# Sparse products of a graph kernel: a ring of 40 gather slots, index columns read in place, one wait per 20 gathers

## What is computed

```python
def prop(z):
    return jax.ops.segment_sum(edge_weight[:, None] * z[src], dst, num_segments=N_SUP)
for i in range(L):                       # L = 5
    z = h @ W[i] + b[i]
    x_start = prop(z)
    xi = h
    for _ in range(RHP):                 # RHP = 5
        xi = (prop(xi) + x_start) / (2.0 + GAMA)
    mean = jnp.mean(xi, axis=0)
    var = jnp.var(xi, axis=0)
    out = gamma[i] * (xi - mean) / jnp.sqrt(var + BN_EPS) + beta[i]
    h = jnp.where(out > 0, out, LEAKY_SLOPE * out)
```

## Time and profile before

| | us |
|---|---|
| median of 3 runs | 13111.46 |
| lowest and highest run | 13095.41, 13116.89 |
| span of the profiled execution, first to last instruction | 11598.4 |
| median less span | 1513.1 |
| first to last start of the 5,000 gathers of the sparse products | 1326.5 to 9009.6 |

### The profile page before, as it was taken

How to read it: one execution, slowest core, us unless ns; L and a number is a source line. 1 busy time by engine, 2 the same in 40 slices (tenths; PEclk the granted TensorE clock), 3 DMA queues, 4 the chain that set the end, 5 groups by cost and what they waited for, 6 DMA issues and landing times. The chain is left out here.

```text
span 11598.4 us, 175759 instructions
## 1 busy us (share of the span) xinstructions
PE 7734.7 (67%) x38121; PEld 5090.7 (44%) x38121; DVE 6797.1 (59%) x24532; ACT 1197.8 (10%) x2596; POOL 7123.4 (61%) x7294
## 2 busy tenths in 40 slices
PE   4633377788777797777877778877779177660090
PEld 2423233357333475333663345743337055560070
DVE  5644655567555576555665556765556666450176
ACT  0122000001000011000010000100000511440005
POOL 5756366663666664666636666456666466766664
PEclk8755555679555697555785556965559578785555
DMA  3133354432444424444334444244543522662106
GB/s 126 44 126 142 91 91 92 92 70 69 92 92 92 90 49 95 91 92 92 61 76 93 92 92 81 58 95 92 91 93 52 178 62 63 174 174 36 24 28 268
DMA packets 1057829, 1076.56 MB, mean 93 GB/s; under 512 B 193805, under 2 KB 913982, under 8 KB 1057648
## 3 DMA queue, kind: packets, MB, share of 16 engines
q0 software_dynamic: 211200, 395.39, 22.0%
q1 hardware_dynamic: 723504, 525.23, 14.3%
q10 hardware_dynamic: 123072, 155.41, 4.3%
HBM read 565.26 MB, written 522.63 MB: 94 GB/s over the span
## 5 line engine op out<-in xcount | busy, mean ns | idle before, releaser
L864 POOL DMA_INDIRECT G<-tab,ridx x5000 | 4746.3, 949 | 3013.2 <-issue 2328.4
L981 PE MATMUL PS<-G,lring 128*1 128x128 f32 x10000 | 2411.0, 361 | 1504.0 <-DMA G<-tab,ridx 1470.1
L356 DVE SCALAR_TENSOR_TENSOR G<-G,whole,PS 1x128 f32<-1x128 f32 (+1 forms) x4050 | 1353.8, 334 | 2568.5 <-PE PS L981 1977.4
L995 PE MATMUL PS<-G,M 128*128 128x128 f32 x10000 | 2780.8, 418 | 45.5 <-DVE G L356 44.0
L995 PEld LDWEIGHTS PS<-G,M 128*128 128x128 f32 x10000 | 2155.6, 274 | 684.6 <-issue 376.4
L981 PEld LDWEIGHTS PS<-G,lring 128*1 128x1 f32 x10000 | 556.1, 85 | 3071.0 <-DMA G<-tab,ridx 2721.0
L377 DVE TENSOR_SCALAR M<-keyrow,keycol,wccol 128x128 f32 (+1 forms) x5004 | 1393.6, 350 | 1.0
L956 ACT COPY big<-PS 128x512 f32 x250 | 146.4, 585 | 7147.2 <-PE PS L991 7147.2
L688 ACT ACTIVATE big<-big,nb,rs 128x128 f32<-128x128 f32 x1564 | 614.8, 479 | 935.4 <-POOL nb L679 911.8
L948 DVE TENSOR_TENSOR Y<-PS,big 128x512 f32<-128x512 f32 x1000 | 679.4, 679 | 0.0
L356 DVE SCALAR_TENSOR_TENSOR carry<-G,whole,PS 1x128 f32<-1x128 f32 (+1 forms) x1350 | 451.2, 334 | 182.0 <-DVE G L356 0.3
(11 more groups left out here) (387 smaller groups left out, 9973.5 us busy)
## 6 DMA issues: line engine op xcount, KB each, us to landing
tab<-Y SPq DMA_DIRECT2D x1250, 256.0 KB, 3.1
G<-tab,ridx POOLq DMA_INDIRECT x5000, 3.3
big<-agg SPq DMA_DIRECT2D x90, 832.0 KB, 6.4
x<-big ACTq DMA_DIRECT2D x60, 832.0 KB, 3.6
big<-x SPq DMA_DIRECT2D x60, 832.0 KB, 4.8
xt_d<-big ACTq DMA_DIRECT2D x30, 858.0 KB, 7.7
x2n<-big ACTq DMA_DIRECT2D x30, 838.5 KB, 3.5
big<-x2n SPq DMA_DIRECT2D x30, 838.5 KB, 5.3
```

Of the source, the lines that this page charges most:

```text
L356: nc.vector.scalar_tensor_tensor(carried if jj == GR else row0(j), row0(j - 1), whole[0:1, bass.ds(tile + jj - 1, 1)], local(jj - 1), ALU. ...
L864: pool.indirect_dma_start(G[:, j, 0:D], None, tab_in(k), bass.IndirectOffsetOnAxis(ap=ridx[:, j:j + 1], axis=0)).then_inc(l_got[j], 16)
L981: nc.tensor.matmul(PS[0:1, CAR, j % GR, :], lring[:, j:j + 1], G[:, j, 0:D], start=True, stop=True).then_inc(l_row, 1)
L995: ins = nc.tensor.matmul(PS[:, SUM + h, j % GR, :], M[:, j, :], G[:, j, 0:D], start=True, stop=True)
```

## The change

`G` gets 40 slots (RG) in place of 8. POOL's program for a product is written out as 200 gathers without a loop: slot and index column are constants, the columns are read from `gidx` itself, and DVE's copy into `ridx` and the semaphore `l_idx` are gone. POOL waits once in 20 gathers, on `l_sum` alone, with a credit of LEAD = 5 groups in place of 2. DVE's and PE's loops now have passes of 40 tiles (10 groups), 5 to a product, in place of 25 passes of 8. Later phases place some of their tiles in the part of `G` that they do not use (`spare`).

```diff
-        G = sb("G", [P, U, D + HEADS])
+        G = sb("G", [P, RG, D + HEADS])
...
-            with pool.Fori(0, IT) as i:
-                for j in range(U):
-                    g = 2 * (r0 + i) + j // GR
-                    steady(pool, g + 1)
-                    if j % GR == 0:
-                        pool.wait_ge(l_idx, g + 1)
-                        pool.wait_ge(l_sum, g + 1)
-                    pool.indirect_dma_start(G[:, j, 0:D], None, tab_in(k), bass.IndirectOffsetOnAxis(
-                        ap=ridx[:, j:j + 1], axis=0)).then_inc(l_got[j], 16)
+            for t in range(T):
+                if t % (RG // 2) == 0:
+                    steady(pool, g0 + t // GR + 1)
+                    pool.wait_ge(l_sum, g0 + t // GR + 1)
+                pool.indirect_dma_start(G[:, t % RG, 0:D], None, tab_in(k), bass.IndirectOffsetOnAxis(
+                    ap=gidx[:, t:t + 1], axis=0)).then_inc(l_got[t % RG], 16)
...
-            with dve.Fori(0, IT) as i:
-                for h in range(2):
-                    g = 2 * (r0 + i) + h
-                    running_sums(dve, g, U * i + GR * h, h, lambda j: G[0:1, j, 0:D],
+            with dve.Fori(0, LI) as i:
+                for q in range(NG):
+                    h, g, tile = q % 2, g0 + NG * i + q, RG * i + GR * q
+                    running_sums(dve, g, tile, 0, lambda j, q=q: G[0:1, GR * q + j, 0:D],
                                  lambda jj: PS[0:1, CAR, jj, :], carry[:, 0:D], l_row, l_ch)
...
-                    nc.vector.tensor_copy(ridx[:, GR * h:GR * h + GR],
-                                          gidx[:, bass.ds(U * i + U + GR * h, GR)]).then_inc(l_idx, 1)
...
-                    dve.wait_ge(l_sum, g + 3)
+                    dve.wait_ge(l_sum, g + LEAD + 1)
...
-            with pe.Fori(0, IT) as i:
-                for h in range(2):
+            with pe.Fori(0, LI) as i:
+                for q in range(NG):
...
-                credit(l_sum, 2)
+                credit(l_sum, LEAD)
```

More of the change, by code:

```diff
@@ L38 @@
 TG = T // 2
+RG = 40
+NG = RG // GR
+LEAD = NG // 2
+LI = T // RG
 TP = T + U
@@ L821, in build @@
         ZB_, HZB = (PA, PA + 1), (PB, PC)
-        l_w, l_wr, l_col, l_base, l_idx, l_mask, l_lr, l_ch, l_row, l_sum, l_ev, l_xt, l_xc, l_yl, l_sq = (
-            sem("l_" + n) for n in "w wr col base idx mask lr ch row sum ev xt xc yl sq".split())
-        l_got = pool_sems("l_got", U)
+        l_w, l_wr, l_col, l_base, l_mask, l_lr, l_ch, l_row, l_sum, l_ev, l_xt, l_xc, l_yl, l_sq = (
+            sem("l_" + n) for n in "w wr col base mask lr ch row sum ev xt xc yl sq".split())
+        l_got = pool_sems("l_got", RG)
         l_tab, l_u, l_h, l_z, l_hz = (sems("l_" + n, 2) for n in "tab u h z hz".split())
@@ L967, in l1_pe @@
         def l1_pe(pe, l, k):
-            r0 = rounds(l, k)
+            g0 = 2 * rounds(l, k)
             last = k == NL - 1
-            with pe.Fori(0, IT) as i:
-                for h in range(2):
[L972 to L977, removed]
+            with pe.Fori(0, LI) as i:
+                for q in range(NG):
+                    h, g, tile = q % 2, g0 + NG * i + q, RG * i + GR * q
+                    gl = 2 * IT * l + NG * i + q
+                    for j in range(GR):
+                        s = GR * q + j
+                        if j == 0:
@@ L978, in l1_pe @@
                             pe.wait_ge(l_lr, g + 1)
                             pe.wait_ge(l_ch, OPS * g + 1)
[L980 to L981 removed]
+                        pe.wait_ge(l_got[s], 16 * (LI * (NL * l + k) + i) + 16)
+                        nc.tensor.matmul(PS[0:1, CAR, j, :], lring[:, GR * h + j:GR * h + j + 1], G[:, s, 0:D],
                                          start=True, stop=True).then_inc(l_row, 1)
[L983 to L984 removed]
+                    for j in range(GR):
+                        s = GR * q + j
+                        if j == 0:
@@ L999, in l1_pe @@
                         pe.wait_ge(l_sq, gl)
-                        node_sums(pe, U * i + GR * (h - 1), 1 - h)
+                        node_sums(pe, tile - GR, 1 - h)
             if last:
@@ L1615, in build @@
         xts = big[:, 0:T * XW].rearrange("p (t f) -> p t f", f=XW)
-        AL = sb("AL", [P, T, HEADS])
+        spare = G[:].rearrange("p s f -> p (s f)")[:, U * (D + HEADS):]
+        AL = spare[:, 0:T * HEADS].rearrange("p (t h) -> p t h", h=HEADS)
         AD = sb("AD", [P, U, HEADS])
@@ L1665, in build @@
         HG = 2 * HEADS
-        ALT = sb("ALT", [TG, 2, HEADS, P])
-        FW = sb("FW", [TG, 2, HEADS, P])
-        pen = sb("pen", [TG, 2, P])
+        ALT, FW = (spare[0:TG, 800 + 1024 * k:1824 + 1024 * k].rearrange("p (g h i) -> p g h i", g=2, h=HEADS)
+                   for k in range(2))
+        pen = spare[0:TG, 2848:3104].rearrange("p (g i) -> p g i", g=2)
         tpen = sb("tpen", [TG, 2, HEADS])
@@ L1677, in _ @@
             def _(dve):
-                a2 = AL[:].rearrange("p t h -> p (t h)")
+                a2 = spare[:, 0:T * HEADS]
                 link(dve, "dve", nc.vector.scalar_tensor_tensor(a2, a2, 0.2, a2, ALU.mult, ALU.max))
```

36 lines of the change are left out of this document (18 added, 18 removed).

## The result

| | before | changed |
|---|---|---|
| median, us | 13112.56 (4 runs, 13095.41 to 13116.89) | 15297.74 (4 runs, 15272.18 to 15304.69) |
| ratio | | 1.1662 [1.1646, 1.1678] |
| span of the profiled execution, us | 11598.4 | 15302.9 |

The forecast was 12,546 us, faster. The kernel became 2,185 us slower, far outside the range. The profiled execution of the changed kernel took 15,304.69 us by the clock of the runs, 1.8 us more than its span. Nothing of 1,513 us lies around it, and that is the first sign of what went wrong.

The account below looks back on a forecast made before the run. The prediction took POOL's issue of gathers in the sparse products as the bound: 13,111 us less 470 (20 products) and 95 (five last products) gave 12,546 us, all else 0; 8-in-10 range about 12,390 to 12,790 us.

Parts of the forecast that it names:

- The base: Sum: the 1,513 us between profiled span and median taken as unchanged, the gain subtracted from the median of 13,111 us.
- PE and DVE are faster than POOL: Products, data at hand: PE 4.2 us a group, DVE 3.6, POOL's four gathers 5.02, so POOL's issue is the bound.
- rival 2: Products: PE and DVE need the 5.48 us a group they take now, so any ring gives 13,111 us; chance 0.04.
- The wait is met when POOL comes to it; I take 0: POOL's wait once in 20 gathers: already met, 0 us; if late each time, 6 us a product.
- The 10.3 us from the last gather of a product to the first of the next stay: Switch between products: landing, last group on PE and DVE, and store form a chain the change does not touch.
- The four products of a layer at 250.5 us, the last at 269.5: Gathers of 20 products from 274 to 250.5 us, 470 us gained; five last ones to 269.5 including turn, 95 us.
- Index column: DVE loses 1,250 index copies, covered by its waits for PE: 0; 90 us in all if DVE were the bound.
- satisfied wait: 190 of 200 gathers lose an already met wait: 0 taken, bounds 0 and 0.23 us a gather, 1,150 us in all.
- loop: POOL's gathers written out without a loop: branches fall at gathers that wait anyway, 0 us.
- rival 1: The gather's 0.30 us gap goes with its wait, PE becomes the bound: 11,896 us; chance 0.06.
- Longer passes on DVE and PE: Jumps back over DVE's 302 instructions, 125 in all, up to 2.74 us each, covered by 8 us of slack: 0.
- The slower rival: Last products: PE falls to its low clock for a share of their 250 groups, up to 13,501 us; chance 0.04.

Follow-up runs that it names:

- b0: Kernel before, unchanged, run again with a profile on a slow chip: 13,093.29 us, span 13,091.5.
- e3: Changed kernel with POOL's wait at every fourth gather in place of every twentieth, slow chip: 13,301.86 us.
- e14: Changed kernel with a wait at every fourth gather and POOL up to nine groups ahead, slow chip: 13,644.31 us, ratio 1.038.
- e10: The file of e3 (changed kernel, wait at every fourth gather) run again on a slow chip: 13,305.3 us.
- a0: Changed kernel, unchanged, run again on a slow chip: 15,043.81 us, ratio 1.1524.
- e16: Changed kernel, unchanged, on the same slow chip as e14: 15,376.86 us, ratio 1.1699.
- e7: Changed kernel with a wait at every fourth gather and POOL held to two groups ahead, quick chip: 11,586.85 us.
- e13: The file of e7 (changed kernel, two groups ahead) on a slow chip: 13,106.38 us, ratio 1.0045.
- e4: Changed kernel with PE counting `l_row` up twice a group in place of four times, quick chip: 11,104.55 us.
- e2: Kernel before without the satisfied wait on three of four gathers, slow chip: 13,044.77 us.
- e1: Changed kernel with the satisfied wait before each gather put back, slow chip: 15,043.28 us, ratio 1.1515.
- e8: The file of e4 (changed kernel, two `l_row` updates a group) on a slow chip: 15,069.0 us.
- e12: Changed kernel with a one-column copy on POOL behind each gather, slow chip: 14,637.17 us, ratio 1.1209.
- e9: The file of e1 (changed kernel, satisfied wait before each gather) run again on a slow chip: 15,026.13 us.

## Why the prediction was wrong

**The base.** The step that failed first is the sum's: "I take what lies around the span as unchanged and set the gain against the median". The difference of 1,513 us was not launch and end, which take 1.8 us. It was mostly idle time inside the stages, which my profile did not have. By the b0 profile the products take 305 and 376 us on average in place of 274 and 277, which is 1,113 us of it. The first gather comes 95 us later, what follows the last one takes 263 us longer, and the turns make up most of the rest. This step did not make the forecast's size wrong by itself, as the runs were its base; it hid that the kernel was bound by something else. A gap of 12% between a span and its runs was a finding, and I used it as a constant.

**"PE and DVE are faster than POOL."** This holds for their own work: 3.8 us a group when nothing holds them, less than the 4.2 that I worked out for the low clock. It fails for the hand-over between them, for which I had no term at all. On a slow chip it limits the kernel before to 6.1 us a group (305 us by 50), against the 5.02 of POOL's issue. A larger ring gained nothing there (e3 and e14), and that alone is rival 2, "PE and DVE need what they take now", with a chance of 0.04.

**"The wait is met when POOL comes to it; I take 0."** This is the term that failed by the most. It was wrong on the slow chips: POOL waited 13.4 and 14.1 us at its 20th gathers, 3,308 us in 200 waits. One wait in 20 gathers was costed for the chance that it is met late, never for what 20 gathers in a row do to the others. e10 against a0, and e14 against e16, put the price of that step at about 1,740 us, and e7 and e13 clear all other parts.

**"The 10.3 us from the last gather of a product to the first of the next stay."** The change does touch that chain. POOL ends a product several groups ahead of PE, and the backlog makes 33 us of it on a slow chip. Of the 1,959 us by which the span of a0 exceeds that of b0, the 20 products take 1,000 from first to last gather, these 20 switches 420, the five last products 361 and the turns behind them 153.

**The four products of a layer at 250.5 us, the last at 269.5.** On the quick chip e4 has 250.75 and 254.8 us from the first gather to the end of the last, and its last products take 267 to 270 us up to the turn. With the switches of 12 to 16.5 us in place of 11, the gain was 496 us where the sum had 565. The 250.5 was right. The last product's closing was right in kind, and PE kept a clock of 0.96. e4 differs from the changed kernel in two updates a group, which changed nothing on a slow chip. The changed kernel itself never ran on the quick chip, so its time there is argued and not shown.

**Index column, satisfied wait, loop: 0 each.** Right by e2 and e1 (the wait) and by e13, at 0.45% for all together. The gap of 0.30 us stays without the wait, so rival 1 fell.

**Longer passes on DVE and PE.** Mostly right. Fetches of instructions grew from 42 to 254 on the page's queue q14:

```profile
q14 instruction: 254, 2.07, 0.0%
```

By the rule that the prediction cites it had every pass end in a fetch. The trace shows them in two products of layer 1 and in one of each later layer (24 to 26 of the 254 packets each, 3 to 5 in most others). In a0 these six take 362 to 375 us, the other products but the last ones 347 to 354. That is what the Trainium skill warns of on the page "Runtime: NRT & Kernel Launch", section "Instruction fetch mechanics". It was no part of the main loss, and no run separated it from other differences between products. With the cover that e4 has on the quick chip only its first product took longer, 258 us in place of 250 to 253. Without it, in e7, the six took 275 to 287 us, the others 270 to 274.

**The slower rival** was PE's clock. It came out slower, but not by that: the clock in the last products is 0.70 here, and 0.77 in b0, both with idle time, and PE is busy for 236 of 453 us. The mechanism that did it was in none of my cases, and 0.04 for "slower" was far too little.

## What to carry to other kernels

Compare the profiled execution's own time with the runs before any sum is made: where they differ by more than a per cent, the profile may show another chip's behaviour, and the missing time can be idle time in the stages, as it was here. Where several engines pass small results on by semaphores, don't let POOL issue a long run of indirect gathers at once. If a deeper ring is wanted, keep a wait at each group: on slow chips e3 was slower than the kernel before by 1.8%, the bursts by 15 to 17%, and only two groups ahead cost next to nothing (e13, 0.45%). And a gain that is measured on one chip (e4: -4.3%) must be measured on a second (e8: +15.4%).

## What the runs showed of the hardware that I had not expected

- Chips, of which one was quick and four slow, differ by 12.5 to 13.3% on the same unchanged kernel (11,601 against 13,054 to 13,145 us), while POOL's gathers (median 945 ns quick, 946 slow) and DVE's running sums (334 ns on both) take the same. The difference lies in how late PE's work is seen by DVE: mean delay 0.60 us with the longest at 0.7 on the one, 0.96 and 5.2 on the other, both for the kernel before.
- On slow chips an unbroken run of gathers makes this much worse. Delays reach 43 us and mostly end within 6 us after the run does. After a burst, with POOL silent, PE does its groups in 3.8 us each. On the quick chip a run of 200 gathers does almost nothing (e4: mean 0.68, longest 9.0).
- It goes one way: in all of a0 PE started no more than 1.5 us after the end of the copy with which DVE opens a group, stalls or not.
- What is behind it stays open. The profile names no wait for it ("issue", "remote"). The number of updates (e8), the satisfied wait (e1, e9) and the length of code (e13) are excluded, the gaps between gathers count for a part (e12), and the burst is shown. Whether the products finish late or only their counts, and whether the gathers' transfers or POOL's own work on them does it, was not tried. Nor is it known that the chip itself is the difference: of DMA semaphore counts the traces of the quick chip keep about 133,000, those of the slow ones 44,000 to 55,000 for the same transfers, and every run here was recorded by the profiler, so that the recording's share in the stalls is open.
